# The turn of x in a state-space layer: from TensorE's transposes to VectorE blocks and a scratch in HBM

## The chip, the cores and the metric

One core of one Trainium2 chip. Times are device microseconds (us) from launch to end. Engines: TensorE (PE; PEld is its weight load), VectorE (DVE), ScalarE (ACT), GpSimd (POOL) and SyncE (SP), which here issues the DMAs.

## The reference, cut to what matters

Four layers act on 1024 tokens of 512 values: linear attention, a mixture of LoRA experts, a Mamba-2 style state-space layer, and a second mixture. Nearly all time goes to the third:

```
proj = hidden @ in_proj_w.T                       # gate 8192, x 8192, B 1024, C 1024, dt 128
x, Bm, Cm = silu(causal_conv4(proj[x, B, C]))     # 128 heads of 64, 8 groups share a B and a C of 128
dt = softplus(proj[dt] + dt_bias);  x_dt = x * dt
Y_diag = ((C @ B.T) * decay) @ x_dt               # within a chunk of 128 tokens
Y_off  = C @ (states of the chunk before, from x_dt and decay)
y = rms(Y_diag + Y_off + D * x) * norm_w * silu(gate);  return y @ out_proj_w.T
```

Four sequences of two chunks give eight token tiles of 128.

## The kernel before, in words

The layer runs over 8 groups (g), each in 16 steps (s): half = s // 8 picks 8 of the group's 16 heads, t = s % 8 the token tile. A unit of 8 heads has 512 channels, four tiles (ct) of 128. Channels lie on partitions in `xc` and `gate`; for the products within a chunk, x must lie with tokens on partitions.

Each engine has its own instruction stream and calls its own `step(g, s, kind)` in the same order; kind is lead (the eight steps ahead of group 0 that prepare it), first, middle or last. Semaphores tie the streams together, and inside a stream all is in program order, so a wait holds whatever is written behind it. PE's order in a step (line 2309):

- `turn(g, s + 1)` (line 2195): four transposes of `xc` into PSUM bank 6, x of the next step. In step 15 the turn of the next group's first step stands behind the projection.
- in an odd step `diag` (line 2207) for both steps of the pair, at line 2217: 8 heads, the weights being 64 columns of `xdt`, the moving operand the masked decay matrix `mt`. A float32 product is two instructions, so a pair of steps has 32.
- `project` (line 2180): one tile of the input projection of this or the next group, three float32r passes over 4 x 2 blocks (helper lines 156 to 158), two tiles in steps 10 and 12. In odd steps `across` (line 2228, products at line 2239) stands between its halves: the weights are 128 columns of `xdd`, for the later chunk's part from the earlier one, and the result goes to bank 6 as well.
- `add_up(g, s - 1)` (line 2243): twelve matmuls of z with the output weights, split into high and low parts (lines 2251, 2252, 2255).

DVE's order in a step (line 1974): `add_out(g, s - 2)` (line 1893) into x, waiting for PE; `make_y` and `make_z` for s - 1 (lines 1951, 1961, 1971); `times_dt(g, s + 1)` (line 1904): it reads the transposes from bank 6, multiplies each head's 64 channels by dt and writes `xdt[:, s % 2]`; the split of W_out (`wo_low`, four operations) where t = 1; the taps of the convolution (line 1882, three operations of 1020 elements) where a tile with a convolution was projected; in odd steps `scale_across`; the mask of step s + 2 (line 1926). Taps fall in steps 2, 3, 5, 6, 10, 12, 13 and 14, two sets in 10 and 12.

ACT evicts the projected tile, splits the weights, computes the decays, squares y, makes the high part of z (`square_and_high`, line 1630) and applies silu once the taps are done (line 1573). POOL makes low parts, sums squares and, at the end of an odd step, multiplies `xdt` of the next even step by the chunk decay into `xdd` (`to_chunk_end`, line 1474). SP loads `mt` rows (line 1356), weight tiles (line 1351), `e` and `unit` (`units` of dt), each behind a wait for the buffer's last reader. In the last group the steps 8 to 15 project nothing, and `diag` is made step by step; there D * x is added by PE (line 2224).

Of the kernel before, what the change touches and what calls it, by code (L numbers as in the profile page):

```python
# [11 lines left out]
P = 128  # L12
# [29 lines left out]
LEAD = 8  # L42
W_BUFS, WO_BUFS, ROW_BUFS = 3, CT, 4
# [13 lines left out]
def mixer_kernel(nc, x_in, wq, bq, wo, mt, z, ffn0, ffn1, w_in, w_dt, par, dt_bias, a_log, w_out, out):  # L57
# [6 lines left out]
    with ExitStack() as ctx:  # L64
# [6 lines left out]
        ecs_dram = nc.dram_tensor("ecs_rows", (SH, SEQS * P), F32, kind="Internal").ap()  # L71
        units_dram = nc.dram_tensor("units", (UNITS, P, UNIT), F32, kind="Internal").ap()
# [17 lines left out]
        with ExitStack() as inner:  # L90
            ssm_block(nc, inner, sems, cleared, w_sems, ssm_norm, x_saved, ident, bank, x, xh, xl, xdt, w_bufs, w_in, w_dt, par, dt_bias,
                      a_log, w_out, ncs_dram, ecs_dram, units_dram, ffn1, out)
# [893 lines left out]
def ssm_block(nc, ctx, sems, cleared, w_sems, n, x_saved, ident, bank, acc, xh, xl, xdt, w_bufs, w_in, w_dt, par, dt_bias, a_log, w_out,  # L986
              ncs_dram, ecs_dram, units_dram, ffn, out):
# [40 lines left out]
    wo_l = sb("wo_l", [P, CT, DIM], F32R)  # L1028

# [114 lines left out]
    x_turned = sem("x_turned")  # L1144
    xdt_ready = sem("xdt_ready")
# [116 lines left out]

    def made_last(kind, s):

        return kind == "last" and s == NT - 1
# [4 lines left out]
    def across_bank(kind, s):  # L1270
# [3 lines left out]
        return 0 if s == STEPS - 1 else 6  # L1274

# [23 lines left out]

    def spread(values):  # L1300
        return values.unsqueeze(2).to_broadcast([P, UH, SP_])
# [30 lines left out]
    with nc.Block() as block:  # L1332
        @block.sync
        def _(sp):
            sp.wait_ge(cleared, 1)
            sp.dma_start(dt_raw, w_dt.rearrange("p k h -> p (k h)")).then_inc(dt_loaded, 16)
            for counted in (clamped, decay_ready, mt_ready, x_turned, xdt_ready, diag_done, y_ready, sq_ready,
# [81 lines left out]
            def step(g, s, kind):  # L1419
# [5 lines left out]
                if own(kind) and t == 2 and (half == 0 or kind != "last"):  # L1425
                    for k in range(WO_BUFS):
                        sp.wait_ge(wo_split, wo_at(g, half, k))
                        load_wo(g + half, 1 - half, k)
                for done in masked_in(kind, s):
                    if ahead(kind, done + ROW_BUFS):  # L1430
                        sp.wait_ge(diag_done, at(g, done))
                        load_rows(g, done + ROW_BUFS)
                for m in EARLY[s] + LATE[s]:
                    if has_tile(kind, m) and has_tile(kind, m + 5):
                        sp.wait_ge(w_split, tile_at(g, m + 2))
                        sp.sem_inc(load_begun, 1)
                        load_tile(g, m + 5)
                for made in made_in(kind, s) + ([s] if made_last(kind, s) else []):
# [15 lines left out]
        def _(pool):  # L1454
# [19 lines left out]
            def to_chunk_end(g, s):  # L1474
# [6 lines left out]
                nc.gpsimd.tensor_tensor(xdd[:].rearrange("p (h c) -> p h c", h=UH),  # L1481
                                        xdt[:, s % 2, :].rearrange("p (h c) -> p h c", h=UH),
# [15 lines left out]
            def step(g, s, kind):  # L1498
# [10 lines left out]
                if s % 2 == 1 and ahead(kind, s + 1):  # L1509
                    to_chunk_end(g, s + 1)  # L1510
# [248 lines left out]
        def _(dve):  # L1759
# [135 lines left out]

            def times_dt(g, s):
                g, s = g + s // STEPS, s % STEPS
                half, t = divmod(s, NT)
# [613 lines left out]
```

## Time and profile before

| | |
|---|---|
| median of 3 runs | 1679.78 us (1677.42 to 1680.82) |
| the profiled execution, its own time | 1681.44 us |
| its span, first to last instruction | 1679.7 us |
| TensorE clock granted, mean | 0.997 of full speed (2.4 GHz) |
| busy: PE, DVE, ACT, POOL | 98%, 74%, 77%, 46% |
| DMA | 98662 packets, 166.61 MB, 30.9% of 16 engines on the main queue |

Busy is the union of an engine's instruction times. A matmul's end is modelled and overlaps the next one's start, so the distance between starts is what tells PE's pace. A group of the layer takes 177.8 us; groups 0 to 6 look alike, group 7 ends in the unpaired steps and the last expert layer.

### The profile page before, as it was taken

What the parts mean: (1) busy time and instruction counts of PE and PEld (TensorE: products, weight loads), DVE (VectorE), ACT (ScalarE), POOL (GpSimd) and SP (SyncE); (2) the same over time, 40 slices, a digit from 0 to 9 for tenths busy, and PEclk for the clock granted to TensorE, in tenths of its full rate; (3) what the DMA queues carried; (4) which work ended last, traced back from release to release, by engine and by line L of the source; (5) the groups of instructions that cost most, each with busy time, mean ns of one, the idle gap of its engine ahead of it and who ended that gap; (6) DMA issues with size and microseconds to landing.
All of it is one profiled execution on the core that took longest, in us unless ns stands there. A gap on an engine that the chain in (4) does not pass through costs nothing.

```text
span 1679.7 us, 27176 instructions
## 1 busy us (share of the span) xinstructions
PE 1643.6 (98%) x9464; PEld 1356.5 (81%) x9464; DVE 1244.7 (74%) x1975; ACT 1286.2 (77%) x2218; POOL 779.2 (46%) x806
## 2 busy tenths in 40 slices
PE   6999999999999999999999999999999999999998
PEld 4888777888888888888888888888888888888876
DVE  5887886777677767677767776776767777767886
ACT  4444559878888788869887788878887889689862
POOL 3565124454445355534544354444454545355470
PEclk9999999999999999999999999999999999999999
DMA  5320343233333323323323232323233333223421
GB/s 172 117 89 1 113 145 113 94 95 92 112 93 107 97 82 122 103 74 97 116 88 116 88 116 88 106 79 113 91 107 97 108 96 114 71 89 109 117 91 51
DMA packets 98662, 166.61 MB, mean 99 GB/s; under 512 B 11648, under 2 KB 49920, under 8 KB 96864
## 3 DMA queue, kind: packets, MB, share of 16 engines
q1 hardware_dynamic: 98528, 164.88, 30.9%
q8 instruction: 77, 1.26, 0.3%
q14 instruction: 57, 0.47, 0.1%
HBM read 158.56 MB, written 6.29 MB: 98 GB/s over the span
## 4 chain that ended last, share of the span: by engine, by line
PE 80%; DVE 5%; ACT 2%; issue 1%; POOL 1%; DVEq 0%; POOLq 0%; ACTq 0%
PE bank L156 15%; PE bank L158 15%; PE bank L157 14%; PE bank L2217 7%; PE bank L2251 7%; PE bank L2252 7%; PE bank L2255 7%; PE bank L2239 3%; PE bank L2203 3%; PE bank L2305 1%; ACT m_mt L1582 1%; DVE m_xc L1882 1%; DVE m_y L1961 1%; DVE m_y L1951 0%; DVE m_gate L1882 0%
## 5 line engine op out<-in xcount | busy, mean ns | idle before, releaser
L156 PE MATMUL bank<-xh,w_h 128*128 128x512 f32 x1152 | 469.1, 407 | 6.2 <-DVE m_xc L1882 3.7
L158 PE MATMUL bank<-xh,w_l 128*128 128x512 f32 x1152 | 452.6, 393 | 0.0
L157 PE MATMUL bank<-xl,w_h 128*128 128x512 f32 x1152 | 449.8, 390 | 0.0
L1489 POOL TENSOR_TENSOR m_z_l<-m_zg,m_z_h 128x512 fp32r<-128x512 f32 x128 | 188.1, 1469 | 472.9 <-ACT m_z_h L1636 472.9
L1582 ACT ACTIVATE m_mt<-m_mt,m_unit 128x128 f32<-128x128 f32 x1024 | 312.3, 390 | 0.0
L1471 POOL TENSOR_TENSOR w_l<-w_raw,w_h 128x512 fp32r<-128x512 f32 x142 | 184.8, 1302 | 265.2 <-ACT w_h L1549 265.2
L156 PEld LDWEIGHTS bank<-xh,w_h 128*128 128x128 f32 x1152 | 217.0, 188 | 57.5 <-issue 17.1
L158 PEld LDWEIGHTS bank<-xh,w_l 128*128 128x128 f32 x1152 | 216.6, 188 | 48.0
L1882 DVE SCALAR_TENSOR_TENSOR m_xc<-bank,m_par_conv,m_xc 128x1020 f32<-128x1020 f32 (+2 forms) x192 | 244.3, 1273 | 14.6 <-ACT m_xc L1561 10.1
L157 PEld LDWEIGHTS bank<-xl,w_h 128*128 128x128 f32 x1152 | 217.2, 189 | 39.7
L1893 DVE TENSOR_TENSOR x<-x,bank 128x512 f32<-128x512 f32 x128 | 87.7, 685 | 202.9 <-PE bank L2255 202.8
L2251 PE MATMUL bank<-m_wo_h,m_z_h 128*128 128x512 f32 x512 | 204.3, 399 | 1.6 <-ACT m_z_h L1636 1.0
L2252 PE MATMUL bank<-m_wo_l,m_z_h 128*128 128x512 f32 x512 | 202.5, 396 | 0.0
L1926 DVE TENSOR_TENSOR m_mt<-m_mt,m_cb 128x1024 f32<-128x1024 f32 x128 | 170.3, 1330 | 17.4 <-ACT m_mt L1587 11.4
L1951 DVE SCALAR_TENSOR_TENSOR m_y<-m_xc,m_par_dn,bank 128x128 f32<-128x128 f32 x480 | 134.4, 342 | 51.9 <-PE bank L2217 51.6
L1573 ACT ACTIVATE m_xc<-m_xc 128x1024 f32<-128x1024 f32 x64 | 68.0, 1062 | 113.0 <-DVE m_xc L1882 112.8
L2255 PE MATMUL bank<-m_wo_h,m_z_l 128*128 128x512 f32 x512 | 138.7, 392 | 0.8 <-POOL m_z_l L1489 0.8
L1587 ACT ACTIVATE m_mt<-m_mt 128x1024 f32<-128x1024 f32 x128 | 135.8, 1061 | 2.1
L2217 PE MATMUL bank<-m_mt,xdt 128*64 128x128 f32 x2048 | 126.8, 276 | 0.0
L2217 PEld LDWEIGHTS bank<-m_mt,xdt 128*64 128x64 f32 x2048 | 110.4, 137 | 13.0 <-issue 13.0
L1587 ACT ACT_TABLE_LOAD x93 | 119.3, 1283 | 1.6
L2251 PEld LDWEIGHTS bank<-m_wo_h,m_z_h 128*128 128x128 f32 x512 | 96.1, 188 | 26.4 <-ACT m_z_h L1636 2.3
(315 smaller groups left out, 2871.4 us busy)
## 6 DMA issues: line engine op xcount, KB each, us to landing
m_mt<-ncs_rows SPq DMA_DIRECT2D x128, 512.0 KB, 4.5
w_raw<-w_in SPq DMA_DIRECT2D x144, 256.0 KB, 2.9
m_wo_raw<-w_out_in SPq DMA_DIRECT2D x64, 256.0 KB, 3.7
m_e<-ecs_rows SPq DMA_DIRECT2D x128, 128.0 KB, 3.5
a_wo_raw<-wo_in SPq DMA_DIRECT2D x8, 1024.0 KB, 4.9
x<-x_in SPq DMA_DIRECT2D x8, 256.0 KB, 5.1
a_wq_raw<-wq_in SPq DMA_DIRECT2D x8, 256.0 KB, 3.2
x_saved<-x SPq DMA_DIRECT2D x1, 2048.0 KB, 7.9
```

What stands on the lines that cost most here:

```text
L156: nc.tensor.matmul(out, ah, bh, start=first, stop=False)
L157: nc.tensor.matmul(out, ah, bl, start=False, stop=False)
L158: return nc.tensor.matmul(out, al, bh, start=False, stop=last)
L1471: nc.gpsimd.tensor_tensor(w_l[:, m % 2, :, :], w_raw[:, m % W_BUFS, :, :], f(w_h[:, m % 2, :, :]), ALU.subtract).then_inc(w_split, 1)
L1489: nc.gpsimd.tensor_tensor(z_l[:, s % 2, :, :], zg[:], f(z_h[:, s % 2, :, :]), ALU.subtract).then_inc(zl_ready, 1)
L1582: last = nc.scalar.activation(mt[:, s % ROW_BUFS, h, :], mt[:, s % ROW_BUFS, h, :], ACT.Relu, bias=own_row)
L1587: nc.scalar.activation(slot, slot, ACT.Exp, scale=-1.0).then_inc(decay_ready, 1)
L1882: ins = nc.vector.scalar_tensor_tensor(out=dst[:, :, back:], in0=src[:, :, 0:length - back], scalar=par_conv[:, w:w + 1], in1=dst[:, :, ba ...
L2217: last = nc.tensor.matmul(bank[row:row + SP_, to_bank, (h // 2) * P:(h // 2 + 1) * P], xdt[:, s % 2, h * SP_:(h + 1) * SP_], mt[:, s % ROW ...
L2251: nc.tensor.matmul(bank[:, sum_bank(g, s), :], z_h[:, s % 2, ct, :], wo_h[:, ct, :], start=ct == 0, stop=False)
L2252: nc.tensor.matmul(bank[:, sum_bank(g, s), :], z_h[:, s % 2, ct, :], wo_l[:, ct, :], start=False, stop=False)
L2255: last = nc.tensor.matmul(bank[:, sum_bank(g, s), :], z_l[:, s % 2, ct, :], wo_h[:, ct, :], start=False, stop=ct == CT - 1)
```

## The change: what it does, and the diff

x is no longer turned by PE. DVE transposes blocks of 32x32 (`turn_blocks`): `xc` of a step, 128 channels x (4 tiles x 128 tokens), goes to `x_blocks`, where a partition holds a token's number inside its block of 32, and the four channel tiles c lie side by side as the innermost elements. SP writes `x_blocks` to a scratch in HBM (2 KB from each partition) and reads it back with four DMAs, one for each 32 tokens, in runs of 512 bytes, into `xdt[:, i % 2]`, so that tokens are on partitions and channels lie as (channel r of 128, tile c of 4). DVE then multiplies by dt in place. `diag` and `across` pick a head or a tile with a step of four elements. DVE turns both steps of the next pair in an odd step, and scales both steps of a pair in the even one; `to_chunk_end` moves from the end of the odd step to the end of the even step that it belongs to. In the last steps of the last group a step is turned two steps ahead and scaled one ahead. Bank 6 is no longer used for x, and the waits of PE for it go.

```diff
+BLOCK = 32
+BLOCKS = P // BLOCK
+XT_BUFS = 4
+        xt_dram = nc.dram_tensor("x_turned_rows", (XT_BUFS, P, BLOCKS, CT * BLOCK), F32, kind="Internal").ap()
+    x_blocks = sb("x_blocks", [P, BLOCKS, BLOCK, CT])
...
+    def turned_in(kind, s):
+        if kind == "last" and s >= NT:
+            return [s + 2] if s + 2 < STEPS else []
+        return [s + 1, s + 2] if s % 2 == 1 and ahead(kind, s + 1) else []
+    def scaled_in(kind, s):
+        if kind == "last" and s >= NT - 1:
+            return [s + 1] if s + 1 < STEPS else []
+        return [s, s + 1] if s % 2 == 0 and own(kind) else []
+    def by_side(channels):
+        return channels.rearrange("p (i r c) -> p i r c", i=2, c=CT)
+    def of_head(channels, h):
+        return by_side(channels)[:, h % 2, :, h // 2]
+    def of_tile(channels, ct):
+        return channels.rearrange("p (r c) -> p r c", c=CT)[:, :, ct]
     def spread(values):
-        return values.unsqueeze(2).to_broadcast([P, UH, SP_])
+        return values.rearrange("p (c i) -> p i c", i=2).unsqueeze(2).to_broadcast([P, 2, SP_, CT])
...
+            def write_x(g, s):
+                g, s = normal(g, s)
+                i = nth(g, s)
+                sp.wait_ge(x_turned, i + 1)
+                sp.dma_start(xt_dram[i % XT_BUFS], x_blocks[:].rearrange("p j e c -> p j (e c)")
+                             ).then_inc(x_written[i % 2], 16)
+            def read_x(g, s):
+                g, s = normal(g, s)
+                i = nth(g, s)
+                sp.wait_ge(x_written[i % 2], 16 * (i // 2 + 1))
+                sp.wait_ge(diag_done, at(g, s - 2))
+                if s % 2 == 0:
+                    sp.wait_ge(xdd_ready, pair(g, s - 2))
+                if i < 2:
+                    sp.wait_ge(n.turned, NT)
+                blocks = xt_dram[i % XT_BUFS].rearrange("(a r) j c -> j r a c", a=BLOCKS)
+                for j in range(BLOCKS):
+                    sp.dma_start(xdt[j * BLOCK:(j + 1) * BLOCK, i % 2, :].rearrange("r (a c) -> r a c", a=BLOCKS),
+                                 blocks[j]).then_inc(x_landed[i % 2], 16)
...
                         load_wo(g + half, 1 - half, k)
+                late_turn = kind == "last" and s >= NT
+                if s % 2 == 0 and (own(kind) and paired(kind, s) or kind == "last" and s == NT):
+                    read_x(g, s + 1)
+                for made in turned_in(kind, s)[:1]:
+                    write_x(g, made)
+                if kind == "lead" and s == STEPS - 1:
+                    read_x(g, s + 1)
                 for done in masked_in(kind, s):
                     if ahead(kind, done + ROW_BUFS):
                         sp.wait_ge(diag_done, at(g, done))
                         load_rows(g, done + ROW_BUFS)
+                    if not late_turn and done % 2 == 0 and ahead(kind, done + 2):
+                        read_x(g, done + 2)
+                    if late_turn and done + 2 < STEPS:
+                        read_x(g, done + 2)
...
                         load_tile(g, m + 5)
+                for made in turned_in(kind, s)[1:]:
+                    write_x(g, made)
...
-                nc.gpsimd.tensor_tensor(xdd[:].rearrange("p (h c) -> p h c", h=UH),
-                                        xdt[:, s % 2, :].rearrange("p (h c) -> p h c", h=UH),
+                nc.gpsimd.tensor_tensor(by_side(xdd[:]), by_side(xdt[:, s % 2, :]),
...
-                if s % 2 == 1 and ahead(kind, s + 1):
-                    to_chunk_end(g, s + 1)
+                if s % 2 == 0 and own(kind):
+                    to_chunk_end(g, s)
...
+            def turn_blocks(g, s):
+                g, s = normal(g, s)
+                half, t = divmod(s, NT)
+                i = nth(g, s)
+                if t == 0:
+                    dve.wait_ge(silu_done, conv_at(g - 1 + half, X_LAST[half]))
+                if i >= 1:
+                    dve.wait_ge(x_written[(i - 1) % 2], 16 * ((i - 1) // 2 + 1))
+                nc.vector.transpose(x_blocks[:].rearrange("p j e c -> p j c e"), xc[:, half, :, t * P:(t + 1) * P].rearrange(
+                    "p c (j e) -> p j c e", e=BLOCK)).then_inc(x_turned, 1)
             def times_dt(g, s):
...
-                dve.wait_ge(x_turned, at(g, s))
-                dve.wait_ge(diag_done, at(g, s - 2))
-                if s % 2 == 0:
-                    dve.wait_ge(xdd_ready, pair(g, s - 2))
...
+                dve.wait_ge(x_landed[i % 2], 64 * (i // 2 + 1))
+                x_sides = by_side(xdt[:, i % 2, :])
+                nc.vector.tensor_tensor(x_sides, x_sides, spread(unit[:, half, t * UH:(t + 1) * UH]),
+                                        ALU.mult).then_inc(xdt_ready, 1)
...
             def step(g, s, kind):
                 half, t = divmod(s, NT)
+                for made in turned_in(kind, s)[:1]:
+                    turn_blocks(g, made)
                 if behind(kind, s - 2):
                     add_out(g, s - 2)
...
                         make_z(g, made)
-                if ahead(kind, s + 1) and s != STEPS - 1:
-                    times_dt(g, s + 1)
+                for made in turned_in(kind, s)[1:]:
+                    turn_blocks(g, made)
+                for made in scaled_in(kind, s)[:1]:
+                    times_dt(g, made)
...
                     scale_across(g, s, kind)
+                for made in scaled_in(kind, s)[1:]:
+                    times_dt(g, made)
...
-            def turn(g, s):
...
-                for ct in range(CT):
-                    last = nc.tensor.transpose(bank[:, 6, ct * P:(ct + 1) * P], xc[:, half, ct, t * P:(t + 1) * P],
-                                               ident[:])
-                last.then_inc(x_turned, 1)
...
-                                            xdt[:, s % 2, h * SP_:(h + 1) * SP_], mt[:, s % ROW_BUFS, h, :],
+                                            of_head(xdt[:, s % 2, :], h), mt[:, s % ROW_BUFS, h, :],
...
-                else:
-                    pe.wait_ge(xdt_ready, at(g, s + 1))
                 for ct in range(CT):
-                    last = nc.tensor.matmul(bank[:, across_bank(kind, s), ct * P:(ct + 1) * P], xdd[:, ct * P:(ct + 1) * P],
+                    last = nc.tensor.matmul(bank[:, across_bank(kind, s), ct * P:(ct + 1) * P], of_tile(xdd[:], ct),
...
             def step(g, s, kind):
-                if ahead(kind, s + 1) and s != STEPS - 1:
-                    turn(g, s + 1)
```

## Rows read from the trace of the kernel before

**Rows 1.** The page, part 1: busy us, share of the span and instructions of each engine.

```profile
PE 1643.6 (98%) x9464; PEld 1356.5 (81%) x9464; DVE 1244.7 (74%) x1975; ACT 1286.2 (77%) x2218; POOL 779.2 (46%) x806
```

**Rows 2.** Busy time by stretch: the second group of the layer, with clock, DMA share, GB/s.

```profile
593.67:771.52 177.85, 177.67 (x1033) 147.04 (x1033) 130.36 (x187) 148.34 (x256) 84.80 (x90) 1.00 0.31 99
```

**Rows 3.** Groups of PEld: count | busy us, mean ns | idle before, releasers.

```profile
L2217 PEld LDWEIGHTS bank<-m_mt,xdt 128*64 128x64 f32 x2048 | 110.4, 137 | 13.0 <-issue 13.0
...
L2239 PEld LDWEIGHTS bank<-m_cb_across,m_xdd 128*128 128x128 f32 x512 | 66.8, 191 | 6.4 <-issue 1.5
L2203 PEld LDWEIGHTS bank<-ident,m_xc 128*128 128x128 f32 x512 | 63.0, 140 | 20.3 <-ACT m_xc L1573 3.8 <-DVE xdt L1904 1.1
```

**Rows 4.** PE's timeline: start us, us, engine, line, operation, count; an even and an odd step.

```profile
613.71 0.60 PE L2203 MATMUL bank<-ident,m_xc 128*128 128x128 f32 x4
614.07 0.48 PE L156 MATMUL bank<-xh,w_h 128*128 128x512 f32 x1
614.38 0.39 PE L157 MATMUL bank<-xl,w_h 128*128 128x512 f32 x1
614.61 0.40 PE L158 MATMUL bank<-xh,w_l 128*128 128x512 f32 x1
...
704.43 0.60 PE L2203 MATMUL bank<-ident,m_xc 128*128 128x128 f32 x4
704.96 1.97 PE L2217 MATMUL bank<-m_mt,xdt 128*64 128x128 f32 x32
706.86 0.50 PE L156 MATMUL bank<-xh,w_h 128*128 128x512 f32 x1
...
709.72 1.06 PE L2239 MATMUL bank<-m_cb_across,m_xdd 128*128 128x128 f32 x8
710.53 0.48 PE L156 MATMUL bank<-xh,w_h 128*128 128x512 f32 x1
```

**Rows 5.** Groups of DVE, columns as in rows 3.

```profile
L1971 DVE TENSOR_TENSOR m_zg<-m_y,m_gate 128x512 f32<-128x512 f32 x128 | 101.7, 794 | 4.4
L1893 DVE TENSOR_TENSOR x<-x,bank 128x512 f32<-128x512 f32 x128 | 87.7, 685 | 202.9 <-PE bank L2255 202.8
L1904 DVE TENSOR_TENSOR xdt<-bank,m_unit 128x512 f32<-128x512 f32 x128 | 87.3, 682 | 15.8 <-issue 9.9 <-PE bank L2203 5.9
```

**Rows 6.** Timelines of DVE, ACT and PE in steps 1 to 3 of the second group.

```profile
631.42 1.88 DVE L1926 TENSOR_TENSOR m_mt<-m_mt,m_cb 128x1024 f32<-128x1024 f32 x1
634.33 0.69 DVE L1893 TENSOR_TENSOR x<-x,bank 128x512 f32<-128x512 f32 x1 [1.02 <-PE bank L2255]
...
638.02 3.89 DVE L1882 SCALAR_TENSOR_TENSOR m_xc<-bank,m_par_conv,m_xc 128x1020 f32<-128x1020 f32 x3
641.83 1.21 DVE L1926 TENSOR_TENSOR m_mt<-m_mt,m_cb 128x1024 f32<-128x1024 f32 x1
...
641.94 1.06 ACT L1573 ACTIVATE m_xc<-m_xc 128x1024 f32<-128x1024 f32 x1 [2.47 <-DVE m_xc L1882]
...
649.76 0.62 ACT L1636 ACTIVATE m_z_h<-m_zg 128x512 fp32r<-128x512 f32 x1
...
651.77 0.40 PE L2251 MATMUL bank<-m_wo_h,m_z_h 128*128 128x512 f32 x1
```

**Rows 7.** DMA: landing times (KB each, median us), SP's waits and its issue timeline.

```profile
m_mt<-ncs_rows SPq DMA_DIRECT2D x128, 512.0 KB, 4.5
w_raw<-w_in SPq DMA_DIRECT2D x144, 256.0 KB, 2.9
...
SPq L1436 <- POOL w_l L1471: 660.6, 100, 10.9
...
644.51 1.21 SPq L1356 DMA_DIRECT2D m_mt<-ncs_rows  x2
```

**Rows 8.** PE's timeline of two of the last steps of the last group.

```profile
1585.24 1.09 PE L2217 MATMUL bank<-m_mt,xdt 128*64 128x128 f32 x16
...
1590.57 1.09 PE L2217 MATMUL bank<-m_mt,xdt 128*64 128x128 f32 x16
```

More of the change, by code:

```diff
@@ L91, in mixer_kernel @@
             ssm_block(nc, inner, sems, cleared, w_sems, ssm_norm, x_saved, ident, bank, x, xh, xl, xdt, w_bufs, w_in, w_dt, par, dt_bias,
-                      a_log, w_out, ncs_dram, ecs_dram, units_dram, ffn1, out)
+                      a_log, w_out, ncs_dram, ecs_dram, units_dram, xt_dram, ffn1, out)
 class Norm:
@@ L986, in ssm_block @@
 def ssm_block(nc, ctx, sems, cleared, w_sems, n, x_saved, ident, bank, acc, xh, xl, xdt, w_bufs, w_in, w_dt, par, dt_bias, a_log, w_out,
-              ncs_dram, ecs_dram, units_dram, ffn, out):
+              ncs_dram, ecs_dram, units_dram, xt_dram, ffn, out):
     def sb(name, shape, dt=F32):
@@ L1144, in ssm_block @@
     x_turned = sem("x_turned")
+    x_written = [sem(f"x_written{i}") for i in range(2)]
+    x_landed = [sem(f"x_landed{i}") for i in range(2)]
     xdt_ready = sem("xdt_ready")
@@ L1336, in _ @@
             sp.dma_start(dt_raw, w_dt.rearrange("p k h -> p (k h)")).then_inc(dt_loaded, 16)
-            for counted in (clamped, decay_ready, mt_ready, x_turned, xdt_ready, diag_done, y_ready, sq_ready,
+            for counted in (clamped, decay_ready, mt_ready, xdt_ready, diag_done, y_ready, sq_ready,
                             sq_summed, z_ready, zh_ready, zl_ready, out_done, acc_added):
@@ L2027, in step @@
                         make_z(g, made)
-                if kind == "lead" and s == STEPS - 1:
-                    times_dt(g, s + 1)
                 if ahead(kind, s + 2):
@@ L2036, in step @@
                     sums_to_scale(0)
-                if s == STEPS - 1 and kind in ("first", "middle"):
-                    times_dt(g, s + 1)
                 if kind == "lead":
@@ L2193, in project @@
                     last.then_inc(proj_done, 1)
-            def turn(g, s):
-                g, s = g + s // STEPS, s % STEPS
-                half, t = divmod(s, NT)
-                if t == 0:
-                    pe.wait_ge(silu_done, conv_at(g - 1 + half, X_LAST[half]))
-                pe.wait_ge(xdt_ready, at(g, s - 1))
-                pe.wait_ge(off_ready, pair(g, s - 2 if s % 2 == 1 else s - 4))
-                for ct in range(CT):
-                    last = nc.tensor.transpose(bank[:, 6, ct * P:(ct + 1) * P], xc[:, half, ct, t * P:(t + 1) * P],
-                                               ident[:])
-                last.then_inc(x_turned, 1)
             def diag(g, s):
@@ L2337, in step @@
                     project(g, m, 1)
-                if s == STEPS - 1 and kind != "last":
-                    pe.wait_ge(cb_across_ready, g + 2)
-                    turn(g, s + 1)
                 if behind(kind, s - 1):
```

8 lines of the change are left out of this document (3 added, 5 removed).

## The prediction

> **What bounds the kernel now.** I read the page's busy times first: TensorE (PE) is busy 98% of the span, far above the rest [rows 1]. Matmul ends are modelled, so I then read one whole group of the state-space layer by stage: 177.85 us, of which PE is busy 177.67 us at a granted clock of 1.00, ScalarE (ACT) 148.34 and VectorE (DVE) 130.36 [rows 2]. The groups look alike but for the last, which ends in the tail. Starts of PE instructions follow one another without a hole in the timeline [rows 4], so PE's own issue rate sets the pace. What leaves PE shortens the span until one of two close followers is late: ACT has 29 us of room in a group, DVE 47 us. DVE's idle time before the accumulation into x is 202.8 us, all of it waiting for PE [rows 5]; that is the cover under which DVE's new work must go.
>
> **What is removed.** 128 turns of x, each of four transposes, 512 in all [rows 3]. Busy times of PE overlap, so I price a turn by starts. In front of the products of a pair of steps it runs from 704.43 to 704.96: 0.53 us. In front of a projection it runs from 613.71 to 614.07, 0.36 us, and the first projection matmul behind it then takes 0.31 us to the next start where 0.23 is usual [rows 4]; the switch back costs 0.08, so 0.44 us. Every pair of steps has one of each: 64 x 0.97 = **62 us off PE's path**. The waits of PE on the dt product, for the bank that both shared, go too; the turns' loads stood behind the dt product 1.1 us in the whole run [rows 3], and I count nothing for it.
>
> **The layout, read by TensorE.** The weights of the products with mt (64 columns, 2048 loads) and of the products across chunks (128 columns, 512 loads) were contiguous and now step by 4 elements, 16 bytes. No row shows such a read. Lower bound: nothing; a gain is excluded, since contiguous is the easiest order. A load's duration grows from 137 ns at 64 columns to 191 at 128 [rows 3]: 0.84 ns a column. The transposes' load takes 140 ns for its 128 columns [rows 3]; with the same fixed part of 83 ns that is 0.45 ns a column. So the read path delivers contiguous words about twice as fast as these loads ask. Upper bound: if a stride of 4 words costs as much as reading all 4, a column takes 4 x 0.45 = 1.8 ns. The loads of 64 columns would then take 115 ns where the products now start every 59 ns (1.90 us for 32, [rows 4]), the loads of 128 columns 230 ns against 101 ns (0.81 us for 8): 2048 x 56 + 512 x 129 ns = 115 + 66 = 181 us. I take the lower end, because the path has shown twice the rate that is asked, and keep both ends. The Trainium skill speaks against the change here: Advanced Engine Details and Errata, Memory Cachelines, says that SBUF lines are 16 bytes and that an access which finds a different line each time is penalised. By that rule the sum comes out near the upper bound, which I price as a rival.
>
> **DVE.** Added: 128 block transposes of 128x512. No row has one. Nearest are one-pass operations of that shape on SBUF operands, 683 to 794 ns [rows 5]; I take 0.69 us, the value of the PSUM-read operations and of the uncrowded ones. Their output steps by 4 elements; if each element then costs two cycles, add 512 more at the slope between the 685 ns for 512 and the 1.21 us for 1024 [rows 5, 6]: 1.22 us. That is the upper end, and below 0.53 us (512 elements at that slope alone) I exclude. The dt product (683 ns, 128 times [rows 5]) now reads SBUF twice in place; the nearest row is the gate product with 794 ns, so +0.11 us, upper end again 1.22. Per group DVE gets 16 x 0.80 = 12.8 us more and stands at 143 of 170 us: not the bound on average.
>
> Locally it is tight. In step 1 of a group the mask ends at 633.30, DVE waits 1.02 us for PE, runs unbroken to the taps' end at 641.91, ACT's silu starts at 641.94, and ACT is busy until the high part of z, begun at 649.76 and 0.62 long, is there 1.39 us ahead of the product that needs it at 651.77 [rows 6]. After the change an odd step has two turns and no dt product (2 x 0.69 - 0.68 = +0.70). PE's release comes 0.53 earlier, so 1.02 becomes a lag of 0.21 us; the deadline comes 0.97 us earlier; 1.39 - 0.97 - 0.21 leaves 0.2. An even step has both dt products, the second behind the taps, so the next step starts later again and its slack is about used up. I put a stall of 0.25 us on each of the four loaded spots of a group (behind the weight split of W_out or behind another step with taps): 1 us a group, **8 us**. At 1.22 us for a turn, 1.06 us more is late at each such spot.
>
> **DMA and SP.** Each step adds one write of 256 KB and four reads of 64 KB, 640 issues beside the present 500 or so. SP needs about 0.6 us to issue one (two in 1.21 us), so 3 us more in a step of 10 us; it waits 660.6 us in total for the weight split alone [rows 7], so it has that time. The queue to watch is what stands behind SP's wait for the written scratch: the next mt rows and weight tile, needed one to two steps later. Both land in 3 to 4.5 us [rows 7]. The round trip is 0.69 + 2.9 (a 256 KB move) + four issues 2.4 + a landing of up to 4.5, some 10.5 us; x is due after 13 us or more (a step of 10 us and DVE's first 3 us in the next), so it is hidden with 2 us over. POOL's product with the chunk decay moves one step later and has until the products across chunks, some 5 us behind its new place. Nothing for these.
>
> In the last eight steps of the last group there is no projection, and a step takes 5.33 us [rows 8]. Two steps less the turns are 9.7 us for the same 10.5 us trip. So x is late by about 0.6 us a step: **5 us**. If the trip costs nothing extra, 0; at a landing 2 us slower, 20.
>
> **Sum.** 1681.4 (the profiled execution; its span is 1679.7) - 62 + 8 + 5 = 1632; the median of the runs is 1.7 us lower, so **1630 us**.
>
> **Rivals.**
> - *DVE becomes the late one.* Turn and dt product at 1.22 us: each of four spots adds 1.06 us for turns and up to 0.5 for the dt product, 8 x 4 x 1.6 = 50 us at worst, some 25 where ACT's waits absorb half: 1655, at worst 1680. For: DVE is unbroken for 9 us at a time; against: it waits over 200 us for PE. The Trainium skill (Vector Engine (DVE) Microarchitecture Reference, section 5.2) reports slower streams when a port does not find two adjacent words; no row here shows one.
> - *Slower: strided weights.* One mechanism: the loads of the products pay for their stride, on PE's path. At 1.8 ns a column 181 us come, 62 go, and DVE's stalls vanish since each step is longer: 1680 - 62 + 181 = **1799 us**; where a column costs 1.4 ns, half way up, 2048 x 31 + 512 x 78 ns = 103 us, and the time is 1721. It decides from the point where the added load time passes the 62 us: about 1.2 ns a column. For: PE has no slack, and these two groups are 2560 instructions. Against: contiguous columns come in 0.45 ns. The rule on 16-byte lines above belongs here.
> - *x comes late in all steps.* If landings under four more issues a step grow by 3 us, diag waits about 1 us per pair: +64 us, 1682, no change.
> - *The change does not do what it says:* the transposes leave PE by the diff, and no other path stays; under 0.01.
>
> **How the numbers follow.** Forecast with hidden DMA and unstrided price 0.36; DVE late 0.15; strided weights 0.42; x late 0.07. The faster cases hold just over half, so the predicted time stands there, and their own range is 1612 (no stall at all, and the switch costs gone) to 1665. The slower case is nearly as likely, and the range must take most of it: 1612 to 1790 leaves out the ends of it and little else, below 0.2. A difference under 0.2% (3 us) is what a measurement can't tell from none: same 0.03, faster 0.53, slower 0.44.
>
> **What would show it.** Right: no transposes in the layer's PE rows, the 32 products of a pair still in 1.90 us and the eight across in 0.81, a middle group of about 171 us with PE busy over 98%, and DVE transposes of about 0.7 us. Wrong: loads of 64 columns at 190 ns instead of 137, groups of 185 us or more with PE still full (strided weights); or PE holes behind the high part of z (DVE), or behind the dt product with DVE waiting for a DMA (x late).

## The result and the profile after

The changed kernel takes 1727.18 us (median of 4 runs, 1725.34 to 1730.7), the kernel before 1678.86 on the same chip (4 runs, 1677.42 to 1680.82): ratio 1.029, interval 1.0267 to 1.0312. It is slower by 48 us where 1630 us and a gain were forecast. The profiled execution took 1725.34 us, 1723.6 of it span.

The page, parts 1 and 2 of the kernel after (the engines, as in [rows 1]; then busy share and granted clock in tenths, in 40 slices):

```profile
PE 1665.1 (97%) x8952; PEld 1378.3 (80%) x8952; DVE 1382.9 (80%) x2103; ACT 1283.8 (74%) x2218; POOL 816.8 (47%) x806
...
PE   6999989999999999999999999999999999999688
...
PEclk9999999999999999999999999999999999999789
```

PE runs 512 instructions fewer and is busy 21.5 us more, and toward the end it is no longer full and its clock falls. So there are two places to look at. The products of B and C within the chunks (line 2305 before, 2370 after) come once a group and cut the trace into groups. Before, six groups took 177.8 us and one 170.0, the last began at 1482.72; after, they take 179.7 to 180.2 and 169.9, and the last begins at 1491.83. So of the 43.9 us between the two profiled executions 9 come before the last group and 35 in and behind it (the tail). The 9 are 12.2 us more over the seven groups, less 3.1 us by which the first group began earlier (242.74 against 245.86). That start varies between 242.7 and 246.0 also among kernels with the old turn (242.66 in experiment 3, 246.02 in experiment 1), so I don't count it as an effect of the change.

Busy time by stretch, columns as in [rows 2], the same stretch of a middle group, and then the last group's start to the end of the span, all of the kernel after:

```profile
593.67:771.52 177.85, 177.71 (x957) 147.67 (x956) 144.34 (x200) 145.51 (x252) 89.21 (x90) 1.00 0.47 144
...
1491.83:1723.60 231.77, 203.56 (x1097) 165.10 (x1096) 162.33 (x275) 135.37 (x250) 92.45 (x103) 0.93 0.36 114
```

The same view of the kernel before, for the second of them:

```profile
1482.72:1679.70 196.98, 190.33 (x1160) 153.53 (x1160) 147.57 (x258) 134.50 (x250) 90.71 (x102) 1.00 0.28 91
```

In the middle PE is as full as before, at full clock, with DVE well below it: PE's own instructions must have grown. In the tail PE has 28.2 us of holes (time in which it does nothing), where it had 6.7, and a mean clock of 0.93.

The loads' groups, as in [rows 3], and PE's timeline of a pair of steps, as in [rows 4], kernel after:

```profile
L2284 PEld LDWEIGHTS bank<-m_mt,xdt 128*64 128x64 f32 x2048 | 128.9, 208 | 30.7 <-issue 29.6
...
L2304 PEld LDWEIGHTS bank<-m_cb_across,m_xdd 128*128 128x128 f32 x512 | 124.3, 325 | 14.6 <-issue 12.0
```

```profile
704.64 2.19 PE L2284 MATMUL bank<-m_mt,xdt 128*64 128x128 f32 x32
706.76 0.50 PE L160 MATMUL bank<-xh,w_h 128*128 128x512 f32 x1
...
709.66 1.91 PE L2304 MATMUL bank<-m_cb_across,m_xdd 128*128 128x128 f32 x8
711.33 0.48 PE L160 MATMUL bank<-xh,w_h 128*128 128x512 f32 x1
```

By starts, the eight products across take 1.67 us instead of 0.81: 209 ns each instead of 101. The 32 products with mt take 2.12 instead of 1.90: 66 ns instead of 59. That is 1.08 us a pair. Eight pairs a group make 8.6 us against the 7.75 us (62 over 8 groups) of the transposes that left; of the 2.0 us by which a group grew, 1.1 are left. Summed over four middle groups of both traces by the distances between starts, the products across cost 6.8 us a group more, those with mt 1.8 more, and what left is 7.45: 6.95 of transposes and 0.5 of the switch back. The other 0.9 us are longer distances among the projection's and the output's matmuls. PE counts as idle for only 0.14 us of most groups, so the rows don't say what these are; I call them stalls.

DVE's groups, as in [rows 5], kernel after:

```profile
L1973 DVE STREAM_TRANSPOSE m_x_blocks<-m_xc 128x512 f32<-128x512 f32 x128 | 144.1, 1126 | 19.3 <-DMA x_turned_rows<-m_x_blocks 17.8
...
L1982 DVE TENSOR_TENSOR xdt<-xdt,m_unit 128x512 f32<-128x512 f32 x128 | 98.8, 773 | 37.5 <-DMA xdt<-x_turned_rows 37.3
```

The turn by blocks takes 1.13 us, not 0.69; the dt product 773 ns. In the tail, the timelines of SP's issues, of DVE around steps 9 and 10 of the last group, of POOL and of PE, kernel after (in brackets the idle time before a row and what ended it):

```profile
1591.32 0.43 SPq L1410 DMA_DIRECT2D x_turned_rows<-m_x_blocks  x1
1598.17 1.24 SPq L1399 DMA_DIRECT2D m_e<-ecs_rows  x2
...
1602.86 0.42 SPq L1438 DMA_DIRECT2D w_raw<-f_bias  x1
1603.39 1.80 SPq L1424 DMA_DIRECT2D xdt<-x_turned_rows  x4
...
1615.75 1.74 SPq L1424 DMA_DIRECT2D xdt<-x_turned_rows  x4
```

```profile
1608.38 0.69 DVE L1982 TENSOR_TENSOR xdt<-xdt,m_unit 128x512 f32<-128x512 f32 x1 [7.97 <-DMA xdt<-x_turned_rows]
...
1611.45 1.13 DVE L1973 STREAM_TRANSPOSE m_x_blocks<-m_xc 128x512 f32<-128x512 f32 x1
...
1619.16 0.69 DVE L1982 TENSOR_TENSOR xdt<-xdt,m_unit 128x512 f32<-128x512 f32 x1 [6.07 <-DMA xdt<-x_turned_rows]
```

```profile
1614.37 1.30 POOL L1551 TENSOR_TENSOR m_xdd<-xdt,m_unit 128x512 f32<-128x512 f32 x1
```

```profile
1609.82 1.99 PE L2284 MATMUL bank<-m_mt,xdt 128*64 128x128 f32 x16 [4.68 <-DVE m_y L2025]
...
1625.37 1.23 PE L2284 MATMUL bank<-m_mt,xdt 128*64 128x128 f32 x16
```

The write of x of step 9 is issued at 1591.32, but SP issues its four reads only at 1603.39, behind the two loads of `e` (for which it waited 6.4 us) and the loads of the experts' weights. DVE waits 8 us for the landing, and PE waits for DVE. Its 16 products then take 1.99 us where this kernel's own at full clock take 1.23. Busy time and clock in the stretch from their first start to the next instruction's (columns as in [rows 2]):

```profile
1609.82:1611.73 1.91, 1.91 (x16) 1.58 (x16) 1.91 (x3) 1.82 (x4) 0.59 (x1) 0.50 0.12 47
```

The granted clock is 0.50 there, the lower level of 1.2 GHz. Means over 10 us from 1600 on are 0.70, 0.67, 0.78 and 0.74: the clock goes to and fro between the two levels, and PE had stood idle for 2.45 us before 1600.56, where it first falls, and for 4.68 us before 1609.82. So a wait is paid a second time in slower instructions.

Step 10 is late for another reason. Its reads overwrite the half of `xdt` from which POOL makes xdd of step 8, so SP waits for xdd. POOL makes it from 1614.37 to 1615.67, and the reads go out at 1615.75. SP's waits for POOL's xdd from the last group's start to the end (us in total, times, the longest):

```profile
SPq L1419 <- POOL m_xdd L1551: 25.6, 4, 9.5
```

PE has 11.2 us of holes, in four places, right ahead of the products across, which read xdd.

### The profile page after: what moved, and what is told of

Read it like the earlier page. It is cut to its first block, busy times and chain, and to the rows that moved or that the text cites. A ratio compares the mean times of both kernels' runs of the same rounds, so it can differ in the third digit from the quotient of the medians.

```text
span 1723.6 us, 26802 instructions
## 1 busy us (share of the span) xinstructions
PE 1665.1 (97%) x8952; PEld 1378.3 (80%) x8952; DVE 1382.9 (80%) x2103; ACT 1283.8 (74%) x2218; POOL 816.8 (47%) x806
## 4 chain that ended last, share of the span: by engine, by line
PE 67%; DVE 10%; ACT 5%; issue 4%; DMA 2%; SPq 1%; POOL 1%; DVEq 0%; ACTq 0%; POOLq 0%
PE bank L160 13%; PE bank L162 12%; PE bank L161 12%; PE bank L2284 6%; PE bank L2316 6%; PE bank L2317 6%; PE bank L2320 6%; PE bank L2304 5%; DVE m_xc L1951 3%; ACT m_mt L1651 2%; DVE m_x_blocks L1973 1%; DVE m_y L2028 1%; PE bank L2370 1%; DMA x_turned_rows<-m_x_blocks 1%; DMA xdt<-x_turned_rows 1%
## 5 line engine op out<-in xcount | busy, mean ns | idle before, releaser
L1558 POOL TENSOR_TENSOR m_z_l<-m_zg,m_z_h 128x512 fp32r<-128x512 f32 x128 | 183.8, 1436 | 491.4 <-ACT m_z_h L1705 491.3
L1541 POOL TENSOR_TENSOR w_l<-w_raw,w_h 128x512 fp32r<-128x512 f32 x142 | 197.5, 1391 | 260.2 <-ACT w_h L1618 260.1
L2316 PE MATMUL bank<-m_wo_h,m_z_h 128*128 128x512 f32 x512 | 208.4, 407 | 8.3 <-DVE m_wo_l L1988 3.6
L2317 PE MATMUL bank<-m_wo_l,m_z_h 128*128 128x512 f32 x512 | 206.2, 403 | 0.0
L2003 DVE TENSOR_TENSOR m_mt<-m_mt,m_cb 128x1024 f32<-128x1024 f32 x128 | 183.5, 1433 | 6.4 <-ACT m_mt L1656 6.0
L1973 DVE STREAM_TRANSPOSE m_x_blocks<-m_xc 128x512 f32<-128x512 f32 x128 | 144.1, 1126 | 19.3 <-DMA x_turned_rows<-m_x_blocks 17.8
L2284 PEld LDWEIGHTS bank<-m_mt,xdt 128*64 128x64 f32 x2048 | 128.9, 208 | 30.7 <-issue 29.6
L2284 PE MATMUL bank<-m_mt,xdt 128*64 128x128 f32 x2048 | 142.2, 291 | 6.3 <-DVE m_y L2025 4.7
L2304 PEld LDWEIGHTS bank<-m_cb_across,m_xdd 128*128 128x128 f32 x512 | 124.3, 325 | 14.6 <-issue 12.0
```

The costliest lines, as they stand in the source:

```text
L1541: nc.gpsimd.tensor_tensor(w_l[:, m % 2, :, :], w_raw[:, m % W_BUFS, :, :], f(w_h[:, m % 2, :, :]), ALU.subtract).then_inc(w_split, 1)
L1558: nc.gpsimd.tensor_tensor(z_l[:, s % 2, :, :], zg[:], f(z_h[:, s % 2, :, :]), ALU.subtract).then_inc(zl_ready, 1)
L2284: last = nc.tensor.matmul(bank[row:row + SP_, to_bank, (h // 2) * P:(h // 2 + 1) * P], of_head(xdt[:, s % 2, :], h), mt[:, s % ROW_BUFS, h ...
L2304: last = nc.tensor.matmul(bank[:, across_bank(kind, s), ct * P:(ct + 1) * P], of_tile(xdd[:], ct), cb_across[:, s % NT // CHUNKS, :], star ...
L2316: nc.tensor.matmul(bank[:, sum_bank(g, s), :], z_h[:, s % 2, ct, :], wo_h[:, ct, :], start=ct == 0, stop=False)
L2317: nc.tensor.matmul(bank[:, sum_bank(g, s), :], z_h[:, s % 2, ct, :], wo_l[:, ct, :], start=False, stop=False)
```

## The experiments

**1. The stride of the products across, alone.** The kernel before, with the columns of each of these loads 4 elements apart:

```diff
-                    ... ct * P:(ct + 1) * P], xdd[:, ct * P:(ct + 1) * P],
+                    ... ct * P:(ct + 1) * P], xdd[:].rearrange("p (r c) -> p r c", c=CT)[:, :, ct],
```

> The kernel before, in which only the products across chunks read their 128 weight columns of xdd with a step of 4 elements; the layout in xdd is not changed with it, so these products mix other channels, and the count and order of instructions stay. Theory 1 (the strided weight load of 128 columns costs 209 ns in place of 101, as the changed kernel's eight products in 1.67 us say): 64 pairs x 0.86 us = 55 us more, about 1734 us, groups of 177.8 + 6.9 = 184.7 us, since PE has no slack. Rival (the longer products in the changed kernel come from their later or slower operand, or from its denser DMA traffic, not from the stride): eight products stay at 0.81 us and the time at 1679.

Measured: 1733.46 us (1728.12 to 1734.36) against 1680.34, ratio 1.0309 (1.0291 to 1.0328). PE's timeline of this kernel:

```profile
705.51 1.91 PE L2239 MATMUL bank<-m_cb_across,m_xdd 128*128 128x128 f32 x8
707.17 0.48 PE L156 MATMUL bank<-xh,w_h 128*128 128x512 f32 x1
```

The 1.66 us are those of the changed kernel, with no other part of the change there. This term alone costs 53 us, 6.6 in each middle group (184.4 us instead of 177.8).

**2. The stride of the products with mt, alone.** The same in the loads of 64 columns:

```diff
-                                            xdt[:, s % 2, h * SP_:(h + 1) * SP_], mt[...],
+                                            xdt[:, s % 2, :].rearrange("p (i r c) -> p i r c", i=2, c=CT)[:, h % 2, :, h // 2], mt[...],
```

> The kernel before, in which only the products with mt read their 64 weight columns of xdt with a step of 4 elements; the layout in xdt is not changed with it, so these products mix other channels. Theory 1 (the loads of 64 columns suffer little, 66 ns in place of 59, because neighbours go to different column halves and overlap): 64 pairs x 0.22 us = 14 us more, about 1693 us. Rival (a strided column costs the same everywhere, some 1.6 ns): 2048 loads at 105 ns in place of 59 give 94 us more, 1773 us.

Measured: 1691.86 us (1690.8 to 1692.91) against 1680.34, ratio 1.0066 (1.0049 to 1.0083). The row of the load is that of the changed kernel:

```profile
L2217 PEld LDWEIGHTS bank<-m_mt,xdt 128*64 128x64 f32 x2048 | 128.2, 208 | 13.0 <-issue 13.0
```

```profile
706.75 2.19 PE L2217 MATMUL bank<-m_mt,xdt 128*64 128x128 f32 x32
708.87 0.50 PE L156 MATMUL bank<-xh,w_h 128*128 128x512 f32 x1
```

A load of 64 strided columns is listed at 208 ns instead of 137, yet products start 66 ns apart instead of 59 (2.12 us for 32). Durations in the rows of loads overlap; only starts give the price. Middle groups take 179.6 us, 1.8 more, which makes 14.6 us for eight. The time rose by 11.5 only: in the profiled executions, which are as far apart, the first group began 2.3 us earlier than in the kernel before.

**3. A step of 2 elements.** As experiment 1, at 8 bytes instead of 16.

> The kernel before, with the weight columns of the products across chunks taken with a step of 2 elements (8 bytes) in place of 1; other channels are mixed. If the cost comes from finding a new 16-byte line at every column, a step of 2 finds two columns in each line: the eight products take between 0.81 and 1.24 us, the time at most 28 us more. If any step other than 1 costs the full price, 1.67 us and about 1734 us, as with a step of 4.

Measured, one run: 1682.59 us.

```profile
707.38 1.09 PE L2239 MATMUL bank<-m_cb_across,m_xdd 128*128 128x128 f32 x8
708.23 0.48 PE L156 MATMUL bank<-xh,w_h 128*128 128x512 f32 x1
```

0.85 us for eight, 106 ns each: a step of 8 bytes costs 5 ns a load, one of 16 bytes costs 108. It isn't being strided that costs. The Trainium skill (Advanced Engine Details and Errata, Memory Cachelines) has lines of 16 bytes; by that rule each column at a step of 4 touches a line of its own, and two share one at a step of 2. These two rows agree with it; which part of the read path does it, no run here shows.

**4. Why 64 columns cost so little.** In the kernel after, the eight heads in the order 0, 2, 4, 6, 1, 3, 5, 7, so that loads which follow one another go to the same half of PE's columns:

```diff
-                for h in range(UH):
+                for h in [0, 2, 4, 6, 1, 3, 5, 7]:
```

> The changed kernel with the heads of the products with mt in the order 0, 2, 4, 6, 1, 3, 5, 7, so that neighbours no longer alternate between the two halves of PE's columns. Theory (strided loads into different halves overlap, and that is why they cost so little): the 32 products of a pair go from 2.12 us to about 32 x 105 ns = 3.4 us, 64 x 1.2 = 79 us more, about 1800 us. Rival (loads of 64 columns are cheap for another reason, whatever the order): 2.12 us and 1727 us as they are.

Measured, one run: 1772.07 us.

```profile
700.86 2.98 PE L2284 MATMUL bank<-m_mt,xdt 128*64 128x128 f32 x32
703.77 0.50 PE L160 MATMUL bank<-xh,w_h 128*128 128x512 f32 x1
```

91 ns a product instead of 66, less than the 105 ns expected. So with strided loads the alternation between the halves is worth 25 ns a product. That it does so by hiding the stride is not shown: contiguous loads in this order weren't run, and part of the 25 ns may belong to the order itself.

**5. The kernel after with contiguous loads.** Both groups of loads read neighbours. The channels are then mixed up, so the output is not the reference's; the work is the same.

> The changed kernel with both kinds of products reading their weight columns contiguously from the same buffers (so heads and channels are mixed; counts and order stay). Theory (the strides cost PE 55 + 14 us, and little of it covered other waits): 1727 - 69 = 1658 us if nothing else is late; DVE has 145 us of work in what would be a group of 171 us and loses some in places: 1658 to 1670, middle groups of 171 to 173 us. Rival (DVE or ACT is the real pace of the changed kernel and the stride hides under it): groups stay at 178 us or more, the time above 1710.

Measured: 1677.55 us (1674.5 to 1680.96, 8 runs), ratio 0.9986 (0.9975 to 0.9998). One group of it:

```profile
593.67:766.40 172.73, 171.02 (x970) 139.70 (x969) 148.59 (x203) 147.37 (x255) 89.45 (x90) 1.00 0.49 151
```

50 us came off, not the 57 to 69 expected. A group took 172.7 us, not 170, and PE had 1.7 us of holes in this stretch of one group's length: with the strides gone the followers are late. So the stalls are 2.4 us a group by the 7.45 us that left, 2.7 by the 7.75 forecast. The last group and what follows still took 31.7 us more than before.

**6. The turn with contiguous writes.** The block transposes write in another order of channels (output again mixed):

```diff
-                nc.vector.transpose(x_blocks[:].rearrange("p j e c -> p j c e"), xc[...
+                nc.vector.transpose(x_blocks[:].rearrange("p j e c -> p (j e c)").rearrange("p (j c e) -> p j c e", j=BLOCKS, c=CT), xc[...
```

> The changed kernel with DVE writing its transposed blocks contiguously into x_blocks in place of a step of 4 elements (the scratch then holds channels in another order). Theory (the transposes take 1.13 us because each element they write is 16 bytes from the last): 0.6 to 0.7 us each, DVE busy 55 us less; since DVE is not on the path in the middle groups, the time falls by less than 10 us. Rival (a transpose of 512 elements takes 1.1 us by itself): 1.1 us and no change.

Measured, one run: 1727.22 us, so no change; its middle groups take 179.3 us where the kernel after has 179.7.

```profile
L1973 DVE STREAM_TRANSPOSE m_x_blocks<-m_xc 128x512 f32<-128x512 f32 x128 | 90.1, 704 | 23.1 <-DMA x_turned_rows<-m_x_blocks 21.8 <-ACT m_xc L1642 1.2
```

The write's step of 16 bytes is what takes 704 ns to 1126. 54 us of DVE's time bought at most 0.4 us a group, so DVE does not set the pace of the changed kernel's middle.

**7. The tail: reads first.** SP issues the read of step 9 ahead of the experts' loads, nothing else.

> The changed kernel with one move: SP issues the four reads of x of step 9 in front of the loads of the last layer's weights (7 DMAs and their two waits), not behind them. In the changed kernel these reads were issued at 1603.39 though the scratch was written long before, and DVE waited 7.97 us for them. Theory (half of the tail's loss is the queue order, the rest the trip itself): PE's hole of 4.7 + 2.5 us and the slow clock behind it go, 8 to 12 us less, about 1717 us. Rival (the trip is late in every step whatever the order): at most 3 us less.

Measured: 1722.26 us (1719.79 to 1722.4), ratio 1.0244 (1.0229 to 1.026): 5 us, between the two expectations; the tail takes 227.7 us instead of 231.8. DVE waits 3.15 us for the landing of step 9 instead of 7.97. The reads still stand behind the two loads of `e`, and steps 10 to 15 keep their waits.

**8. The tail: x turned by PE.** The above, and steps 10 to 15 of the last group turned by PE as in the kernel before. These steps then have the old layout too, so their products read neighbours again. By the rows above that saves three sets across at 0.86 us and six times 0.14 us (1.23 against 1.09 of [rows 8]), 3.4 us, and the six turns cost about as much, 2.6 to 3.2 us at 0.44 to 0.53 (an estimate). So the gain is that of the trip.

```diff
+    def by_pe(g, s):
+        return g == LAST and s >= NT + 2
```

> The changed kernel, but in the last six unpaired steps of the last group (10 to 15) x is turned by PE into bank 6 and scaled from there, as in the kernel before; and SP reads x of step 9 ahead of the loads of the last layer's weights. Theory (35 of the 44 us between the profiled executions lie behind the last group's start, because x makes its round trip between the products of one step and those of the step after next, and PE's clock falls in the holes): the stretch from the last group's products within the chunk (1491.8) to the end goes from 231.8 us to 197 plus some 3, so 1727 - 32 = 1695 us, with the clock back at 1.00. Rival (the tail is late because the whole pipeline of DVE is late by then): it stays within 5 us of 1727.

Measured: 1711.14 us (1710.97 to 1712.19) against 1680.48, ratio 1.0183 (1.0168 to 1.0198). Both together give 16 us, half of the 32 expected. From the last group's start to the end 216.4 us are left, 19 more than before, though in its second half nearly all x is turned as it was. DVE now waits for POOL's xdd itself, 10.3 us in all.

**9. Contiguous xdd with the right output.** POOL, which makes xdd anyway, writes it tile by tile, so that the products across read neighbours. Only the product with mt still reads with a stride:

```diff
-        return channels.rearrange("p (r c) -> p r c", c=CT)[:, :, ct]
+        return channels[:, ct * P:(ct + 1) * P]
...
-                nc.gpsimd.tensor_tensor(by_side(xdd[:]), by_side(xdt[:, s % 2, :]),
-                                        spread(unit[:, half, first:first + UH]), ALU.mult).then_inc(xdd_ready, 1)
+                nc.gpsimd.tensor_tensor(xdd[:].rearrange("p (c i r) -> p c i r", i=2, c=CT),
+                                        xdt[:, s % 2, :].rearrange("p (i r c) -> p c i r", i=2, c=CT),
+                                        spread4(unit[:, half, first:first + UH]), ALU.mult).then_inc(xdd_ready, 1)
```

> The kernel after, but GpSimd writes its scaled x (xdd) tile by tile, so that the eight products across chunks read 128 weights that lie next to each other; VectorE's part and the head-by-head products still read every fourth number. The output is the same. Theory of the stride: eight products back from 1.67 us to about 0.82, 64 times, so about 54 us less; as the version with all weights contiguous fell by 50 us and its head-by-head products stand for some 8 to 14 of these, this one falls by 38 to 46 us and gives about 1685 us (1680 to 1692); the row of the products reads 0.8 us for eight. GpSimd's product may change from 1.38 us either way, it is not waited for in the middle. Rival, that the regained time is taken up again by waits of VectorE for the turned x: 1695 or more. Loss of the tail stays (some 230 us from the last group's start to the end).

Measured: 1687.28 us (1682.76 to 1688.97), ratio 1.0044 (1.003 to 1.0057): 40 us less, as expected. A group takes 174.0 us.

**10. Experiments 8 and 9 together.**

> The edit above, and the last group's steps 10 to 15 turned by TensorE again, with the read of step 9 ahead of the experts' loads. The output is the same. If the two losses add up, the 16 us that the tail edit gave alone come off again: about 1669 us (1664 to 1676), faster than the kernel before (1680) by some 0.6%. Rival: with the middle faster, the tail's edit gives less or the products across find GpSimd late: 1680 or more.

Measured: 1670.52 us (1668.44 to 1671.77), ratio 0.9946 (0.9933 to 0.9958): the two gains add up, and this version beats the kernel before. Its DVE timeline shows what still holds the tail:

```profile
1568.89 0.68 DVE L1978 TENSOR_TENSOR x<-x,bank 128x512 f32<-128x512 f32 x1
1573.20 0.69 DVE L2001 TENSOR_TENSOR xdt<-bank,m_unit 128x512 f32<-128x512 f32 x1 [3.62 <-POOL m_xdd L1566]
```

DVE waits for POOL's xdd of step 8, which reads the same half of xdt. POOL's own timeline:

```profile
1568.58 1.52 POOL L1574 TENSOR_TENSOR m_z_l<-m_zg,m_z_h 128x512 fp32r<-128x512 f32 x1 [3.73 <-ACT m_z_h L1721]
...
1571.80 1.26 POOL L1566 TENSOR_TENSOR m_xdd<-xdt,m_unit 128x512 f32<-128x512 f32 x1
```

POOL stood idle for 3.73 us ahead of that z and made xdd only behind it and its squares, though DVE had scaled x of step 8 at 1555.94. That is the change's move of xdd to a later step, whose cost I had put at nothing.

**11. POOL's old place in the tail.** In the last group's second half xdd is made at the end of the step before, on top of experiment 10:

```diff
+                early = kind == "last" and s >= NT - 1
+                if s % 2 == 1 and early and s + 1 < STEPS:
+                    to_chunk_end(g, s + 1)
-                if s % 2 == 0 and own(kind):
+                if s % 2 == 0 and own(kind) and not early:
                     to_chunk_end(g, s)
```

> The kernel of the version with contiguous xdd and a tail turned by TensorE (1670.52 us), with one edit: in the last group's second half GpSimd makes its scaled x (xdd) at the end of the step before, as in the kernel before, and not behind the squares of its own step. Same output. Theory: the rest of the tail's loss is this move, since VectorE waited 6.4 + 3.6 us for xdd before it wrote the next x, and TensorE 10.3 us in four holes ahead of the products across; both vanish and the time falls by 8 to 11 us, to about 1661 (1658 to 1664). Rival, that the late landing of step 9's x holds the chain and the rest only shifts: 3 us or less, 1667 or more.

Measured: **1657.5 us** (1656.05 to 1660.61) against 1679.14, ratio 0.9877 (0.9859 to 0.9895): 13 us off, two more than the upper expectation. The last group and what follows, in this kernel:

```profile
1454.65:1654.70 200.05, 187.96 (x1120) 150.77 (x1120) 157.65 (x269) 135.66 (x251) 96.09 (x103) 1.00 0.36 116
```

200.0 us against 197.0 before, and the clock is back at 1.00.

**12. Step 9 by PE as well**, on top of 11.

> The edit above, and step 9 of the last group turned by TensorE as well (its write and its read go). Same output. VectorE's wait of 4.2 us for the landing of step 9's x goes: another 3 to 5 us off if the chain runs through it, so about 1657 us (1653 to 1660), 1.4% below the kernel before; rival, that the wait only moves to the next operation (TensorE's transposes come in its place, or GpSimd): within 1.5 us of the version above.

Measured: 1656.71 us (1654.42 to 1658.67), ratio 0.9866 (0.9851 to 0.9881): 0.8 us, within both runs' spread. The rival held: DVE's wait of 4.20 us for step 9's landing is gone, but it now waits 3.65 us for step 8's, where experiment 11 has 2.06, and 2.13 us for ACT's decays. The tail takes 198.3 us.

**13. POOL's order alone, in the kernel after.**

> The kernel after with the one edit of GpSimd's order in the last group's second half, nothing else. Same output. The tail's loss (34.8 us) came off in three parts in the versions with contiguous xdd: x turned by TensorE and the read put ahead gave 16, GpSimd's order 13, step 9 about 1. If the two causes are independent, this order alone gives about 13 us here too: 1714 (1711 to 1717). If they are not, because with x coming through HBM the landing of x ends the wait last anyway and xdd's readiness only lets the read of the next even step start sooner, it gives 2 to 8 us: 1719 to 1725. TensorE's 11.2 us of holes ahead of the products across should shrink in either case.

Measured: 1712.94 us (1710.76 to 1714.33) against 1680.76, ratio 1.019 (1.0172 to 1.0208): 14 us off, as expected; the tail takes 216.4 us instead of 231.8. The same view of SP's waits has:

```profile
SPq L1419 <- POOL m_xdd L1551: 6.8, 3, 3.6
```

and PE's holes ahead of the products across are gone. So the late xdd is a cause of its own in the changed kernel. It acts through both: these products, and the next even step's reads of x, wait for it.

## Why the prediction was wrong

**The strided loads are the step that failed.** I took their lower end, nothing. Of the two bounds, the 66 us for the products across came true nearly whole (0.86 us for each of 64 pairs, 55 us; 53 by the run), the 115 us for the products with mt did not (0.22 us a pair, 14 us; 11.5 by the run). The reason I gave, that contiguous columns come in 0.45 ns where the loads ask for 0.84, compared listed durations, which experiment 2 shows not to be the price, and could at best show a spare rate for neighbours. At a step of 16 bytes the across loads add 108 ns over 128 columns, 0.84 ns each. The rule I had cited against the change held in sign, and its rival came out at about 65 us, not 181. The 128 columns cost nearly what I had as the upper end (209 ns a product for 230). The 64 columns cost 66 ns where I had 115, and 91 without the alternation between the halves, which I had left out; why even that is below 115 stays open.

The 1727 us lie inside my range of 1612 to 1790 only because I stretched it to take in this rival; the forecast's own mechanism reached to 1665. The mark by which I wanted to know the rival misled in part: the loads of 64 columns are listed at 208 ns, as it said, but these were the cheap ones, and a middle group takes 180 us, not 185 or more.

**The tail.** I had 5 us, at most 20; it was 35. Even the 5 did not follow from my rows: a trip of 10.5 us against 9.7 is 0.8 us in two steps, not 0.6 in each. Two terms were missing. Experiments 7 and 8 show the late x: 16 us. The trip itself was shorter than forecast (8.2 us for step 8, from DVE's turn at 1585.77 to the dt product at 1593.96). I saw neither what stands before the reads in SP's queue nor how one late step slows the next at a lower clock. Experiment 13 shows the other, 14 us for POOL's later xdd. I had checked the move against the products across alone, and for the middle of the run. In the tail xdd stands behind a z that is itself late, and both the products across and the next even step's reads of x wait for it.

The tail's length in the traces splits the 35 us in the order in which the experiments took them off: 231.8 us in the kernel after, 227.1 with contiguous xdd (9), 210.7 with the old turn in steps 10 to 15 (10), 200.1 with POOL's old place (11), 198.3 with step 9 (12), against 197.0 before. So 4.7 us of the tail are the products' stride, 16.4 the late x, 10.6 the late xdd and 1.8 step 9; 1.3 stay unexplained. The sizes depend on the order: alone in the kernel after, experiments 8 and 13 each took 15.4 us off the tail.

**The removal held.** I had 62 us, 7.75 a group; by starts over four middle groups it is 7.45, so some 60.

**DVE and stalls.** The turn took 1126 ns; I had taken 0.69, which is the contiguous one's 704, and 1.22 as the upper end. The dt product took 0.77 for 0.79. I had 1 us of stalls a group. In the changed kernel it is 0.9 to 1.1, but there PE is slow enough to hide more; with the strides gone it is 2.4 to 2.7, some 11 to 13 us more than forecast. That DVE sets the pace of the middle is refuted by experiment 6.

**DMA and SP in the middle** cost nothing that PE shows: it is busy 177.71 of 177.85 us. The rival in which x comes late in all steps is out with it; its price of 64 us should also have read 1694, as it left my own 8 + 5 us out of the sum.

**The sum.** Between the profiled executions: -3.1 (the first group's start) + 12.2 (seven groups) + 34.8 (the tail) = 43.9. The medians are 48.3 apart, and the runs of the kernel after spread over 5.4 us. From the terms of the forecast it is -62 + 53 + 11.5 + about 9 of stalls + 35 = 46.5; this counts some 1.5 us of the last group twice, in the 35 and in the terms for all groups.

## What to carry to other kernels

Work that a change hands to TensorE through the layout of its operands counts as much as work that it takes away: price each weight load by the distance between the starts of products, and where a tile is rewritten anyway (here by GpSimd), let that write restore neighbours. Check every moved instruction in the last stage of the pipeline apart, where nothing is left to cover it: who reuses its operand's buffer, and what stands ahead of it in its queue. The change, so mended and with six steps given back to PE's turn (experiment 11), gains 1.2% where it lost 2.9%.

## What the runs showed of the hardware

- Weight loads of 128 columns, 4-byte elements: a product every 101 ns with neighbours, 106 with a step of 8 bytes (one run), 209 with a step of 16.
- Loads of 64 strided columns: 66 ns a product where they alternate between the halves of TensorE's columns, 91 where four heads in a row go to one half (one run), 59 for neighbours in alternation.
- VectorE's transpose by blocks of 32, 128x512: 704 ns into neighbours, 1126 into a step of 16 bytes.
- Around and after the holes of step 9 the granted clock was 0.67 to 0.78 in the mean of each 10 us for some 40 us, going between 1.2 and 2.4 GHz, and 16 products took 1.99 us instead of 1.23. With the holes closed (experiment 11) its mean over the last group and what follows was 1.00.
